# One product of the second batch ahead of the first output tiles, and the last accumulation ahead of the last but one output tiles

## What is computed

```python
xn = layernorm(x)
s  = causal_attention(xn @ WQ, xn @ WK, xn @ WV)
# feed-forward, N = 4096 tokens, 8 experts, two per token:
routed_in  = xn[flat_idx] * weights
h          = silu(grouped(routed_in, w1)) * grouped(routed_in, w3)
routed_out = grouped(h, w2)
shared     = silu(xn @ sw1.T) * (xn @ sw3.T) @ sw2.T
out        = shared.at[flat_idx].add(routed_out)     # flat_idx holds EXPERT numbers 0..7
g = silu(out)
result = x + s * g
```

## Time and profile before

| | us |
|---|---|
| median of 3 runs | 235.4 (235.35 to 235.5) |
| the profiled execution, own time | 234.9 |
| its span, first to last instruction | 232.8 |
| PE busy in the span | 223.8 (96%) |
| DVE busy | 183.6 (79%) |
| ACT busy | 150.3 (65%) |
| granted PE clock, whole span | 1.00 |

### The profile page before, as it was taken

The page is one execution under the profiler, slowest core; times in us unless marked ns, Lnnn a source line. Parts: engine busy times, 40 slices in busy tenths (PEclk is TensorE's granted clock), DMA queues, the critical chain, the costliest instruction groups (busy, mean ns, idle before and its releaser), DMA issues.

```text
span 232.8 us, 4647 instructions
## 1 busy us (share of the span) xinstructions
PE 223.8 (96%) x1500; PEld 199.8 (86%) x1500; DVE 183.6 (79%) x618; ACT 150.3 (65%) x403; POOL 67.0 (29%) x120
## 2 busy tenths in 40 slices
PE   6899999999999999999999999899999999999983
PEld 5788899998998998989989988798888989889743
DVE  3878659799798898897699897778686776769765
ACT  2454755856856747658557674697869686788712
POOL 5321732853656538529020200002020120202000
PEclk9999999999999999999999999999999999999999
DMA  5699520020200200001000000129754638384322
GB/s 173 205 326 303 171 93 1 5 88 8 73 17 8 90 4 6 1 8 34 0 3 1 0 4 0 48 32 220 201 84 147 122 103 183 74 197 71 112 86 96
DMA packets 19319, 19.78 MB, mean 85 GB/s; under 512 B 1176, under 2 KB 18272, under 8 KB 19296
## 3 DMA queue, kind: packets, MB, share of 16 engines
q1 hardware_dynamic: 16128, 16.35, 23.2%
q0 software_dynamic: 3168, 3.15, 9.1%
HBM read 15.15 MB, written 4.34 MB: 84 GB/s over the span
## 4 chain that ended last, share of the span: by engine, by line
PE 91%; DVE 3%; ACT 2%; DMA 2%; issue 1%; SPq 1%; DVEq 0%; ACTq 0%
PE bank L440 83%; PE bank L535 4%; PE bank L489 3%; DMA raw_qkv<-in_L_attn_WK 2%; ACT arena L779 1%; DVE raw_sw L1476 1%; DVE w L1474 1%; DVE arena L1016 1%; PE bank L623 1%; ACT w L945 0%; PE bank L462 0%; DVE arena L1401 0%; SPq L233 0%; ACT xT_hi_all L779 0%; ACT probs L779 0%
## 5 line engine op out<-in xcount | busy, mean ns | idle before, releaser
L440 PE MATMUL bank<-xT_hi_all,arena 128*128 128x512 f32 (+3 forms) x256 | 78.8, 365 | 0.7 <-DVE arena L1016 0.7
L440 PE MATMUL bank<-arena 128*128 128x256 f32 (+1 forms) x496 | 69.3, 285 | 0.8 <-DVE arena L1016 0.7
L440 PEld LDWEIGHTS bank<-arena 128*128 128x128 f32 (+1 forms) x496 | 62.8, 182 | 5.5 <-DVE arena L1016 1.8
L440 PEld LDWEIGHTS bank<-xT_hi_all,arena 128*128 128x128 f32 x256 | 46.8, 188 | 6.9 <-DVE arena L1016 0.9
L779 ACT ACTIVATE arena<-bank 128x512 fp32r<-128x512 f32 (+4 forms) x83 | 36.0, 455 | 24.7 <-PE bank L440 23.3
L1016 DVE TENSOR_TENSOR arena<-bank,arena 128x264 fp32r<-128x264 f32 (+4 forms) x83 | 41.5, 509 | 12.7 <-ACT arena L779 12.4
L440 PE MATMUL bank<-xT_lo_all,arena 128*128 128x512 f32 (+3 forms) x128 | 45.9, 358 | 0.0
L431 POOL DMA_DIRECT2D x_ring<-in_L_attn_x x6 | 7.9, 1316 | 71.3 <-DVE x_ring L1411 71.3
L440 PEld LDWEIGHTS bank<-xT_lo_all,arena 128*128 128x128 f32 x128 | 24.2, 189 | 2.2
L809 ACT ACTIVATE probs<-bank,neg_max 128x128 f32<-128x128 f32 (+3 forms) x32 | 17.0, 531 | 13.0 <-DVE neg_max L1074 12.9
L1401 DVE SCALAR_TENSOR_TENSOR arena<-w,w_rows,arena 128x128 fp32r<-128x128 f32 x64 | 18.2, 346 | 6.7 <-ACT arena L779 6.7
(11 more groups left out here) (132 smaller groups left out, 398.1 us busy)
## 6 DMA issues: line engine op xcount, KB each, us to landing
x_ring<-in_L_attn_x SPq DMA_DIRECT2D x7, 512.0 KB, 3.5
x_ring<-in_L_attn_x POOLq DMA_DIRECT2D x6, 512.0 KB, 5.9
out<-x_ring SPq DMA_DIRECT2D x6, 512.0 KB, 3.3
spread<-pairs SPq DMA_DIRECT2D x14, 128.0 KB, 3.6
w_sb<-in_L_ffn_w SPq DMA_DIRECT2D x1, 1024.0 KB, 11.2
raw_sw<-in_L_ffn_sw SPq DMA_DIRECT2D x3, 256.0 KB, 4.4
x_ring<-in_L_attn_x SPq DMA_DIRECT2D x2, 256.0 KB, 3.0
xn<-in_L_attn_x SPq DMA_DIRECT2D x1, 512.0 KB, 6.5
```

The source lines that it names most:

```text
L440: return nc.tensor.matmul(dst, lhsT, rhs, start=start, stop=stop, skip_group_check=True, **kw)
```

## The change

Two edits.

1. PE: `hidden(1,1,1)` moves from the end of `step2(1)` to directly behind `gather(0,1)`, ahead of the cleared accumulator and of `shared_out(0,0)`.
2. Batch 7: PE takes `accumulate(7,1)` ahead of `shared_out(6,1)` rather than behind it. ACT takes `rows_high(7,1)` ahead of `silu_out(6,0)`, and DVE `rows_low(7,1)` ahead of `gate_attn(6,0)`. The routed output and the first of the last output tiles go to `h1_bank[0]` in place of `o_bank`; the wait for `gate_done` goes, and one for `h_mult_done` (`h1_bank[0]` has then been read out) comes.

```diff
@@ routed_out
-                mm(o_bank[:, 0:D], zero_bf[:, 0:P], zero_bf[:, :], True, False)
+                mm(h1_bank[0][:, 0:D], zero_bf[:, 0:P], zero_bf[:, :], True, False)
                 pe.wait_ge(s["pairs_ready"], 1)
                 for g in range(E):
-                    mm(o_bank[0:8, 0:D], pair_out[:, g * 8:(g + 1) * 8], w2_sb[:, g, :], False, False)
+                    mm(h1_bank[0][0:8, 0:D], pair_out[:, g * 8:(g + 1) * 8], w2_sb[:, g, :], False, False)
@@ PE, batches 0 and 1
             gather(0, 1)
+            hidden(1, 1, 1, h3_bank, "h3_done")
             pe.wait_ge(s["pairs_kept"], 1)
@@ PE, step2
                 gather(i, 1)
-                hidden(i, 1, 1, h3_bank, "h3_done")
+                if i > 1:
+                    hidden(i, 1, 1, h3_bank, "h3_done")
                 accumulate(i - 1, 1)
@@ PE, batch 7
             accumulate(i, 0)
+            accumulate(i, 1)
             shared_out(i - 1, 1)
-            accumulate(i, 1)
-
+
+            pe.wait_ge(s["h_mult_done"], C * B - 1)
             pe.wait_ge(s["sum_ready"], 1)
             nc.tensor.transpose(bc_bank[:, 0:PAIRS], sum_w[0:PAIRS, :], ident[0:PAIRS, 0:PAIRS]).then_inc(s["sum_turned"], 1)
-            pe.wait_ge(s["gate_done"], 2 * i)
             routed_out()
             pe.wait_ge(s["h_lo"], C * B)
             pe.wait_ge(s["rows_silu"], RB * B)
-            for t, dst in enumerate((o_bank, acc_bank, g_bank, bc_bank)):
+            for t, dst in enumerate((h1_bank[0], acc_bank, g_bank, bc_bank)):
@@ ACT, batch 7
             silu_rows(i, 1)
+            rows_high(i, 1)
             silu_out(i - 1, 0)
-            rows_high(i, 1)
@@ DVE, batch 7
             rows_low(i, 0)
+            rows_low(i, 1)
             gate_attn(i - 1, 0).then_inc(s["gated"], 1)
-            rows_low(i, 1)
             h_mult(i, 1)
```

More of the change, by code:

```diff
@@ L654, in shared_out @@
                 for u in range(2):
-                    ins = out_tile(2 * half + u, o_bank[:, u * D:(u + 1) * D], onto=i == B - 1 and u == 0)
+                    ins = out_tile(2 * half + u, o_bank[:, u * D:(u + 1) * D], onto=False)
                 ins.then_inc(s["o_done"], 1)
@@ L1004, in _ @@
             h_high(i, 1)
-            for t, src in enumerate((o_bank, acc_bank, g_bank, bc_bank)):
+            for t, src in enumerate((h1_bank[0], acc_bank, g_bank, bc_bank)):
                 act.wait_ge(s["last_tile_done"], t + 1)
```

## The result

Over 20 runs of each, the changed kernel takes 235.69 us at the median (235.32 to 236.15), the kernel before 235.38 (234.9 to 235.74). The ratio of the two is 1.0020, with a 95% interval of 1.0014 to 1.0026: slower by 0.3 to 0.6 us. The forecast was 235.6 (+0.2), in a range of 234.95 to 236.05.

The account below looks back on a forecast made before the run. PE was taken as the bound, except in batch 1's step, where ACT is nearly full. Edit 1 at +0.55 and edit 2 at -0.38 gave +0.17 on 235.4: 235.57, rounded 235.6 us, range 234.95 to 236.05.

Parts of the forecast that it names:

- That edit 1 costs time: Batch 1's step: the moved product delays `gather(1,0)`, which feeds ACT, so `shared_out(1,0)` starts late; +0.55 us (0.50 to 0.60).
- the clearing matmul: PE, batch 1's step, ahead of `shared_out(0,0)`: the 256-column bf16 matmul was put at 0.11 us.
- The hole ahead of `shared_out(1,0)`: PE, batch 1's step: through with its work at about 159.3, PE stands for about 1.9 us until `h_low(1,1)` ends.
- That edit 2 gains 0.38: End of the second part: the transpose starts 0.33 to 0.42 us early, taken as 0.38.
- The wait it adds: PE, batch 7: `accumulate(7,1)` stands for 0.64 us until DVE's `rows_low(7,1)` ends.
- The bank at nothing: Batch 7's routed output in another bank: costed at nothing, with -0.1 to +0.1 us kept.
- edit 1 at no cost: Rival, batch 1's step: ACT has slack or another semaphore releases `silu_rows(1,0)`; `shared_out(1,0)` starts as before, 235.0 us; chance 0.12.
- the slower one: Rival, end of second part: `accumulate(7,1)` is released late and edit 2 gives nothing; 235.95 to 236.1 us; chance 0.13.
- the faster one: Rival: edit 2 wins the whole 0.67 us and edit 1 costs nothing; 234.7 us; chance 0.06.
- The granted clock: Rival: PE's clock falls in batch 1's new 1.9 us hole, a loss of 1.4 us, 237.0 us; chance 0.04.
- The signs of being wrong: `shared_out(1,0)` at 160.6 or before, the reduction before `h_mult(7,1)` is over, or the clock under 1.00 after 159.
- the second sign: DVE, end of second part: the prediction is wrong if the reduction starts before `h_mult(7,1)` is over.

## Why the prediction was right, and where it was off

- **That edit 1 costs time**: right in its mechanism, step by step. `gather(1,0)` 0.64 us ahead of `silu_rows(1,0)`, the whole delay handed down to `h_low(1,1)`, and a hole on PE in place of the old ones. Half the product moved, the gather moved and the order changed each confirm one link.
- **Its size**: forecast +0.55 (0.50 to 0.60), measured +0.69, outside the stated bounds. The mis-sized term is the clearing matmul. The sum had it at 0.11 us, the pace of such matmuls among themselves, and let it begin at the pace of the product. Where it stands it is dearer: the last matmul of the product passes in 152.14 - 151.82 = 0.32 instead of 0.23, and it itself takes 152.37 - 152.14 = 0.23. Product and clearing matmul together take 152.37 - 150.61 = 1.76 us where the sum had 1.46 + 0.11 = 1.57. The gather took 0.39, the lower of its two values, so the sum's own figure was 0.50, and with the missing 0.19 it is the 0.69. In the kernel before the matmul's own 0.23 is hidden in the hole, but the 0.10 on its neighbour was there to be read: the gather ahead of it takes 0.49 and the one at 155.42 takes 0.39. The sum took this for a spread of the gather; I took the row that was easiest to divide instead of asking what stands on either side of it.
- **The hole ahead of `shared_out(1,0)`**: forecast about 1.9 us (161.17 - 159.3), found 161.78 - 159.79 = 1.99 less the 0.23 of the last matmul, 1.76. Its end came 0.14 later than forecast, and its start 0.25: PE was through with its work at 160.02, less the 0.47 of the start 159.55, where the prediction had 159.3 without a working.
- **That edit 2 gains 0.38** (0.33 to 0.42): measured 0.37. The wait it adds was forecast at 0.64, found 1.09 - 0.47 = 0.62. The reduction comes 0.48 early by its distance (221.51 - 161.78 against 220.83 - 160.62), 0.06 more than forecast, and this is given back since PE is busy with `shared_out(6,1)` until the transpose. That PE and DVE reach the transpose nearly together is what the two runs at the end show: freeing DVE alone brings nothing, freeing both 0.21. PE alone was not freed.
- **The bank at nothing**: right only because both parts came together. With the old bank the new order would have had no gain.
- **The rivals**: edit 1 at no cost, and the slower one (a late release of `accumulate(7,1)`), are refuted by d1 and d2, and so is the faster one. The granted clock stayed at 1.00 (2.4 GHz) through the hole of 1.61 us, as these rows of busy times of the changed kernel show (PE alone, then clock), and the 16 matmuls behind the hole take 163.78 - 161.78 = 2.00 us, as the 16 from 152.37 to 154.37 do, ahead of which PE has no hole:

```profile
160.00:162.00 2.00, 0.39 (x2) 1.00 0.83 288
162.00:166.00 4.00, 4.00 (x30) 1.00 0.87 143
```

  The rule of the Trainium skill cited above (page "TensorE: Matmul & The Clock Gate", Part 1) has a throttled clock as the default and activity as what releases it. The trace doesn't contradict it: a hole of this length left the clock up.
- **The signs of being wrong**: `shared_out(1,0)` did not start as early as before, and the clock column reads 1.00 from 159 to the end. The reduction starts at 221.51 and `h_mult(7,1)` is over at 220.91 + 0.69 = 221.60, so by its words the second sign came, by 0.09 us; but neighbouring DVE steps overlap by as much in the kernel before (`rows_low(7,1)`, 218.44 + 1.14, and `h_mult(7,1)`, 219.50). The sign should have asked for a reduction ahead of the start of `h_mult(7,1)`.
- **The total**: +0.17 forecast, +0.32 by the distances, +0.31 by the medians. By the ratio, 0.0020 (0.0014 to 0.0026), it is 0.33 to 0.61 us, so the true difference lies about where 0.2% was said to be the limit of what can be told: it was called "no change", and with 20 runs it is a small loss.

## What to carry to other kernels

A hole in the busiest engine is worth filling only if the stage's next wait isn't set by another engine: look which chain released the engine at the next wait, and whether the filled-in work stands ahead of that chain's feed. Here the same move cost 0.69 us, and gained 0.66 once the gather that feeds ACT came earlier and three steps of ACT and DVE stood behind the ones that PE waits for. Where two engines reach a point together, a faster one alone may bring nothing, as DVE's did here; and a reordering that delays the reader of a buffer needs a second look at who writes it next.

## What the runs showed of the hardware

- One 256-column bf16 matmul between float matmuls costs 0.32 us of PE's time (0.09 on the one before it, 0.23 on itself), where among its like it takes 0.107. With the old bank the clearing matmul of the tail takes 222.92 - 222.70 = 0.22 for itself too. Whether it is the type, the change of weights or the semaphore wait that stands ahead of it isn't shown.
- A 256-column float matmul of the output tiles is followed by the next after 0.12 us, but after 0.22 when it is the first behind a wait of PE (161.78, 162.00 in the changed kernel). The first one behind the bf16 matmul takes 0.22 too (152.37, 152.59).
- The profiles of these 13 kernels, all alike up to `gather(0,1)`, have it between 149.46 and 150.57 us. In the changed kernel's profile the delay was there by the first transposes, which waited for WK to land. Behind `gather(0,1)`, d1 agrees within 0.01 us among kernels with the same order in batch 1's step, and d2 within 0.02 among those with the same end, but for the kernel whose `shared_out(1,0)` starts without a wait (60.61); the two with split output tiles have 60.49 and 60.44. So small edits were told apart by distances in one profile each better than by the medians of a dozen runs.
- The granted clock stayed at 1.00 through a hole of 1.61 us on PE.
